# Channel mix of the skip path as 64-row products on both row halves of TensorE, with a new order of TensorE's and ScalarE's slots

## The reference

```
x_ft = rfft2(h); keep 12 x 12 low modes at both ends of the rows
x1 = irfft2(einsum("bixy,ioxy->boxy", x_ft, w))      # spectral path
x2 = einsum("bchw,oc->bohw", h, conv_w) + conv_b     # skip path: the channel mix
h  = layer_norm(x1 + x2); gelu in all but the last layer
```

## Time and profile before

| | us |
|---|---|
| median of 3 runs | 5614.82 (5611.42 to 5615.45) |
| the profiled execution | 5614.13 |
| its span in the trace | 5612.4 |
| stem phase, slots of `both`, head phase | up to about 810, 810 to 3280, 3280 to 4870 |
| attention and experts | 4900 to 5612 |

### The profile page before, as it was taken

The page is one execution under the profiler, slowest core; times in us unless marked ns, Lnnn a source line. Parts: engine busy times, 40 slices in busy tenths (PEclk is TensorE's granted clock), DMA queues, the critical chain, the costliest instruction groups (busy, mean ns, idle before and its releaser), DMA issues.

```text
span 5612.4 us, 134635 instructions
## 1 busy us (share of the span) xinstructions
PE 5147.1 (92%) x43556; PEld 2927.0 (52%) x43556; DVE 3916.8 (70%) x7712; ACT 3875.5 (69%) x6261; POOL 647.3 (12%) x959
## 2 busy tenths in 40 slices
PE   5878889999999999999999999999999999778778
PEld 2444456666666666666666644433333333334443
DVE  4877888888888888888888865555555554354454
ACT  5888776888666888666888666677777777523333
POOL 0133100233000333000332000000000000000000
PEclk9998899999999999999999999999999999878888
DMA  1334468667687667777676753221111111000000
GB/s 64 129 137 140 138 180 237 225 226 236 213 231 231 226 228 225 232 224 239 222 226 225 229 134 84 57 59 53 53 47 51 53 51 51 8 4 4 7 7 4
DMA packets 398465, 756.32 MB, mean 135 GB/s; under 512 B 246065, under 2 KB 304818, under 8 KB 332602
## 3 DMA queue, kind: packets, MB, share of 16 engines
q1 hardware_dynamic: 378170, 704.04, 39.4%
q0 software_dynamic: 19968, 48.01, 3.8%
HBM read 397.49 MB, written 354.42 MB: 134 GB/s over the span
## 4 chain that ended last, share of the span: by engine, by line
PE 70%; DVE 9%; ACT 8%; issue 7%; SPq 3%; DMA 3%; ACTq 1%; DVEq 0%
PE ps_y L926 10%; PE ps_t L938 8%; PE ps_t L1032 8%; PE ps_t L947 6%; PE ps_f L926 6%; PE ps_y L918 5%; PE ps_f L1017 4%; PE ps_s L903 3%; PE ps_t L1041 2%; PE ps_s L963 2%; DMA big<-hstore 2%; PE ps_t L353 2%; ACT wslot L1211 2%; PE ps_y L892 2%; PE ps_y L1002 2%
## 5 line engine op out<-in xcount | busy, mean ns | idle before, releaser
L1338 DVE TENSOR_REDUCE big<-big 128x16 f32<-128x512 f32 x1280 | 854.0, 675 | 685.3 <-ACT big L1176 681.0
L1331 DVE TENSOR_TENSOR big<-big 128x512 f32<-128x512 f32 x1280 | 938.7, 764 | 30.5 <-DVE big L1360 18.9
L1176 ACT ACTIVATE big<-ps_y 128x512 f32<-128x512 f32 x892 | 545.8, 612 | 482.7 <-PE ps_y L926 425.5
L938 PE MATMUL ps_t<-ident,big 128*128 128x128 f32 x5120 | 809.2, 281 | 55.2 <-DVE big L1331 25.1
L1192 ACT ACTIVATE big<-ps_t,g_now 128x512 f32<-128x512 f32 x1024 | 821.8, 803 | 12.1 <-PE ps_t L938 11.7
L926 PEld LDWEIGHTS ps_y<-conv_now,big 128*128 128x128 f32 x5088 | 616.3, 191 | 362.7 <-issue 362.7
L1185 ACT ACTIVATE big<-ps_t 128x512 f32<-128x512 f32 x1024 | 633.1, 618 | 212.8 <-PE ps_s L963 145.3
L938 PEld LDWEIGHTS ps_t<-ident,big 128*128 128x128 f32 x5120 | 576.1, 143 | 346.8 <-issue 304.6
L947 PE MATMUL ps_t<-ident,big 128*128 128x128 f32 x4096 | 655.5, 283 | 87.1 <-ACT big L1185 84.8
L926 PE MATMUL ps_y<-conv_now,big 128*128 128x128 f32 x5088 | 717.0, 284 | 0.0
L947 PEld LDWEIGHTS ps_t<-ident,big 128*128 128x128 f32 x4096 | 459.4, 143 | 282.0 <-issue 148.9
(11 more groups left out here) (197 smaller groups left out, 7238.6 us busy)
## 6 DMA issues: line engine op xcount, KB each, us to landing
hstore<-big SPq DMA_DIRECT2D x256, 1024.0 KB, 4.1
big<-hstore SPq DMA_DIRECT2D x256, 1024.0 KB, 5.3
xmodes<-x_out SPq DMA_DIRECT2D x128, 312.0 KB, 4.4
y_kt<-ymodes SPq DMA_DIRECT2D x512, 78.0 KB
ymodes<-y_st SPq DMA_DIRECT2D x192, 144.0 KB, 2.5
ymodes<-y_st SPq DMA_DIRECT2D x64, 192.0 KB, 3.3
w_raw<-in_tok_w1r POOLq DMA_DIRECT2D x128, 72.0 KB, 4.5
w_raw<-in_tok_w2r POOLq DMA_DIRECT2D x128, 72.0 KB, 4.4
```

The source lines that it names most:

```text
L938: last = nc.tensor.transpose(ps_t1[:, 128 * b:128 * b + 128], y_sb[2 * k + wh][:, 128 * b:128 * b + 128], ident[:, :])
L1176: af(y_sq[wh], of[:, wh, :], ACT.Square).then_inc(s["sq_done"], 1)
L1331: v_.tensor_tensor(groups(y_sb[2 * k + wh]), groups(y_sb[2 * k + wh]), rstd[:, k // 2, at:at + 16].unsqueeze(2).to_broadcast([128, 16, 32] ...
L1338: v_.tensor_reduce(ss[:, k // 2, at:at + 16], groups(y_sq[wh]), AX.X, ALU.add).then_inc(s["ss_done"], 1)
```

## The change

The channel mix is cut along the diagonal blocks of `conv_now`. `conv(pair, k, step, both)` now handles both units of a slot in two steps. In step 0 unit 0 is multiplied on rows 0 to 63 and unit 1 on rows 64 to 127, in step 1 the other way round. Each product has a 64 x 128 stationary and 64 moving columns and writes the matching 64 columns of its block. So within a step the two row halves write to two banks, and the two products of a block stand one behind the other in the program. Step 1 waits on a new semaphore `conv_half` for the end of step 0, and both `y_done` of a slot rise in step 1.

The slots' order changes with it. TensorE, with `both`: odd slots step 0, TB0, step 1, TO0, inv_w, [mode mix], TB1, TO1, [fwd_w]; even slots TB0, TO0, inv_h, TB1, step 0, TO1, step 1, fwd_h. ScalarE: even slots px0, gelu0, px1, gelu1, square0, keep0, square1, keep1; odd slots px0, gelu0, [sign_w2], square0, px1, gelu1, keep0, square1, keep1, [sign_w1, sign_w2]. `h_px` gets six buffers for four, and px waits for an earlier fwd_h. In head slots step 0 stands where conv 0 stood, and step 1 behind fc2(v,0) instead of behind fc2(v,1).

```diff
@@ -54,7 +54,7 @@
         h_new = [carve(2048) for _ in range(2)]
         y_sb = [carve(512) for _ in range(8)]
         y_sq = [carve(512) for _ in range(2)]
-        h_px = [carve(512) for _ in range(4)]
+        h_px = [carve(512) for _ in range(6)]
         ss, rstd = (carve(128).rearrange("p (j n) -> p j n", j=2) for _ in range(2))
         var, nt = carve(64), carve(64)
         t_w = carve(2048).rearrange("p (j n) -> p j n", j=2)
@@ -122,7 +122,7 @@
             "const_in", "const_zero", "fc0_center", "fc0_copied", "fc0_stored", "fc0_placed", "conv_center", "conv_placed",
             "pads_zero", "fc1_shift", "x_loaded", "x_ready", "x_turned", "x_copied", "conv_ready", "g_ready", "bias_ready",
             "h_loaded0", "h_loaded1", "h_stored0", "h_stored1", "y_loaded", "xmodes_stored", "ymodes_stored",
-            "y_done", "sq_done", "y_read", "ss_done", "norm_step", "xhat_done", "t1_done", "act_done", "t2_done",
+            "y_done", "conv_half", "sq_done", "y_read", "ss_done", "norm_step", "xhat_done", "t1_done", "act_done", "t2_done",
             "px_done", "f_done", "tw_done", "fw_done", "fw_read", "xout_done", "iw_done", "iw_read",
             "x_low", "x_high", "first_low", "first_high", "mix_done", "mix_sum", "mix_read", "w_raw", "w_zero", "w_scaled", "w_added",
             "xt_done", "fc1_done", "g1_done", "fc2_done", "g2_done", "fc3_done", "tok_done", "tok_stored0", "tok_stored1")}
@@ -328,6 +328,10 @@
         def y_of(odd, both):
 
             return ps_f if both and odd else ps_y
+
+        def px_room(k):
+
+            return 2 if k % 2 else 2 * k
 
         s_flat, f_flat = (t[:, :, :].rearrange("p a n -> p (a n)") for t in (ps_s, ps_f))
 
@@ -919,13 +923,21 @@
                                z_kx[j][r, :].rearrange("p (o w) -> p o w", w=32)[:, :, 16 * odd:16 * odd + 16],
                                start=True, stop=False)
 
-            def conv(k, wh, both):
-
+            def conv(pair, k, step, both):
+
+
+                if step == 1:
+                    wait(pe, "conv_half", pair + 1)
                 for b in range(4):
-                    at = 512 * (2 * (k % 2) + wh) + 128 * b
-                    last = mm(y_of(k % 2, both)[:, wh, 128 * b:128 * b + 128], h_in[k // 2][:, at:at + 128], conv_now[:, :],
-                              start=False, stop=(b == 3))
-                last.then_inc(s["y_done"], 1)
+                    for wh in range(2):
+                        r = slice(64 * (wh ^ step), 64 * (wh ^ step) + 64)
+                        at = 512 * (2 * (k % 2) + wh) + 128 * b
+                        last = mm(y_of(k % 2, both)[:, wh, 128 * b + r.start:128 * b + r.stop], h_in[k // 2][r, at:at + 128],
+                                  conv_now[r, r], start=False, stop=(b == 3 and step == 1))
+                        if b == 3 and step == 1:
+                            last.then_inc(s["y_done"], 1)
+                        elif b == 3 and wh == 1:
+                            last.then_inc(s["conv_half"], 1)
 
             def turn_out(unit, kind, k, wh, tok_before):
 
@@ -960,7 +972,7 @@
                         for image in range(2):
                             half, at = image ^ odd, 64 * image + 32 * wh
                             r = slice(64 * half, 64 * half + 64)
-                            last = mm(to[at:at + 32, odd, :], c_fwh[r, :], h_px[2 * odd + wh][r, :], start=True, stop=True)
+                            last = mm(to[at:at + 32, odd, :], c_fwh[r, :], h_px[px_room(2 * j + odd) + wh][r, :], start=True, stop=True)
                 last.then_inc(s["f_done"], 1)
 
             def fwd_w(m, iw_count, g1_count):
@@ -1072,8 +1084,12 @@
                     if inner:
                         head_slot(n, k, pair, turned, front, back2, kind, nxt, mixed, visit)
                         continue
+                    if both and k % 2 == 1:
+                        conv(4 * i + k, k, 0, True)
                     if back1 in STORED:
                         turn_back(turned - 2, k, 0)
+                    if both and k % 2 == 1:
+                        conv(4 * i + k, k, 1, True)
                     if kind is not None:
                         turn_out(turned, kind, (k + 1) % 4, 0, 0)
                     if front == "stem":
@@ -1084,10 +1100,6 @@
                         if isinstance(q, int) and q == 0 and k == 0:
                             pe.wait_ge(s["conv_ready"], ph)
                             wait(pe, "tw_done", 2 * n - 3)
-                        if k == 0:
-                            fwd_h(n - 2, 1, ps_s, 0, 2 * i + 1, 0, 0)
-                        if k == 2:
-                            fwd_h(n - 1, 0, ps_s, 0, 0, n - 1, 0)
                         if k % 2 == 0:
                             wait(pe, "mix_read", mixed)
                             inv_h(n, k, True)
@@ -1097,15 +1109,20 @@
                             inv_w(n + 1, 0, 0, 2 * n - 1, ps_s)
                         if visit is not None:
                             mix(*visit, ps_y, 2 * (4 * n + k))
-                        conv(k, 0, True)
                     if back1 in STORED:
                         turn_back(turned - 1, k, 1)
+                    if both and k % 2 == 0:
+                        conv(4 * i + k, k, 0, True)
                     if kind is not None:
                         turn_out(turned + 1, kind, (k + 1) % 4, 1, 0)
+                    if both and k % 2 == 0:
+                        conv(4 * i + k, k, 1, True)
+                        if k == 0:
+                            fwd_h(n - 2, 1, ps_s, 0, 2 * i + 1, 0, 0)
+                        else:
+                            fwd_h(n - 1, 0, ps_s, 0, 0, n - 1, 0)
                     if k == 1 and back2 in STORED and both:
                         fwd_w(n - 2, 2 * i + 2, 0)
-                    if front in MIXED:
-                        conv(k, 1, True)
                     if k == 1 and back2 in STORED and front == "stem":
                         fwd_w(n - 2, 0, 0)
                     if k == 2 and nxt in MIXED and front == "stem":
@@ -1139,14 +1156,14 @@
                 if not opening:
                     fc3(pair - 1, 2 * pair + 2)
                 if front is not None:
-                    conv(k, 0, False)
+                    conv(4 * i + k, k, 0, False)
                 fc2(v, 0)
+                if front is not None:
+                    conv(4 * i + k, k, 1, False)
                 fc1(v + 1, 1, iw_later, mixed if visit is None else mixed + visit[5])
                 if kind is not None:
                     turn_out(turned, kind, (k + 1) % 4, 0, pair)
                 fc2(v, 1)
-                if front is not None:
-                    conv(k, 1, False)
                 fc2(v + 1, 0)
 
             turn_x(0)
@@ -1182,7 +1199,7 @@
             def px(unit, k, wh, half):
                 act.wait_ge(s["t2_done"], unit + 1)
                 wait(act, "f_done", half)
-                af(h_px[2 * (k % 2) + wh], ps_t2[:, :], ACT.Copy).then_inc(s["px_done"], 1)
+                af(h_px[px_room(k) + wh], ps_t2[:, :], ACT.Copy).then_inc(s["px_done"], 1)
 
             def gelu(unit, m, k, wh, kind):
                 act.wait_ge(s["t1_done"], unit + 1)
@@ -1258,9 +1275,30 @@
                             square(unit + 1, 1, ps_y)
                             keep_y(unit + 1, k, 1, ps_y)
                         continue
+                    if front in MIXED and back1 in STORED:
+                        of = y_of(k % 2, True)
+                        px(turned - 2, k, 0, 2 * (n - 1) + (k - 1) // 2)
+                        if kind in STORED:
+                            gelu(turned, m, kt, 0, kind)
+                        if slots is not None and k == 3:
+                            sign_w2(ph, q - 8, slots[1], 1)
+                        if k % 2 == 1:
+                            square(unit, 0, of)
+                        px(turned - 1, k, 1, 2 * (n - 1) + (k - 1) // 2)
+                        if kind in STORED:
+                            gelu(turned + 1, m, kt, 1, kind)
+                        if k % 2 == 0:
+                            square(unit, 0, of)
+                        keep_y(unit, k, 0, of)
+                        square(unit + 1, 1, of)
+                        keep_y(unit + 1, k, 1, of)
+                        if slots is not None and k == 1:
+                            sign_w1(ph, q - 8, bass.ds(4 * q - 8 * 4 if slots[0] == 0 else 4 * q - 16 * 4, OCH), slots)
+                            sign_w2(ph, q - 8, slots[0], 0)
+                        continue
                     for wh in range(2):
                         if back1 in STORED:
-                            px(turned - 2 + wh, k, wh, 2 * (n - 1) + k // 2)
+                            px(turned - 2 + wh, k, wh, 2 * (n - 1) + (k - 1) // 2)
                         if kind in STORED:
                             gelu(turned + wh, m, kt, wh, kind)
```

## The result

The changed kernel takes 6356.5 us (median of four, 6333.4 to 6364.6) against 5613.2 us, a ratio of 1.132 (95% interval 1.129 to 1.135). The forecast was slower, which it is, but at 6136 us, and 6356 lies above its range of 5880 to 6300. The profiled execution has a span of 6359.4 us, 747 more than before's; 522 had been forecast.

What follows compares the result with a forecast made beforehand. TensorE, busy 92% and nearly gapless in the layers, was taken to bound the kernel. Scaling quads 219, other quads 127, head 126 and clock 50 sum to 522 us on 5614.13: 6136 us, range 5880 to 6300.

Steps and rivals of the forecast that it cites:

- The product: Channel mix step: 16 loads of 64x128 weights cost 0.89 us, as before, both halves loading at once; saving 0.
- rivals 1 and 2: Mix steps, 1: loads halve like streams, 5636 us, chance 0.05; 2: tiles also drain in half the time, 5480, chance 0.07.
- rival 3: Mix steps: the halves don't run at once, +0.89 us on each of 1024 steps, about 7000 us; chance 0.04.
- The chain and the shapes: Layer slots: waits of the new order and tile-shape changes, +219 us in 48 weight-scaling quads, +127 us in 49 others.
- the long wait: TensorE before TB1 of slot 2 in weight-scaling quads: px0 stands behind ScalarE's scaling block, 2.3 us.
- bare quad: Layer quad without weight scaling after the change: two halves of 13.32 us, 26.64 us in all.
- the small scaling: ScalarE in slot 3 of a scaling quad, ahead of the square: adds 0.25 us.
- shape changes: TensorE in layer quads: more switches between matmul tile shapes, 2.4 us a quad, 0 if waits hide them.
- The head: 124 head slots: y done later and fc2 waits for ScalarE, +1.0 us a slot, +126 us; between 0 and 1.2 a slot.
- The clock: Scaling quads: TensorE's wait lowers its granted clock, 1 us a quad, +50 us; up to +163 us.
- the bound of 3.4 a quad: Scaling quads: most clock loss allowed, from 6.8 us at 0.50 seen after one stem wait, 3.4 us a quad.
- the walk: Layer slots timed instruction by instruction along the new order: a scaling quad takes 29.2 us against 24.6.

Runs made afterwards that it cites:

- half-columns run: Changed kernel with each split product streaming 32 of its 64 columns, half of the channel mix's output columns left out, loads unchanged: 6335.2 us, 1.130.
- the order alone: Changed kernel's TensorE slot order and ScalarE order, with whole 128-row products where the split steps stood: 5944.7 us, 1.060 of the kernel before.
- the run with the wait taken away: Changed kernel with ScalarE's scaling block moved from the end of slot 1 to behind gelu 0 of slot 2: 6000.4 us, 1.069.
- the products alone: Kernel before, its slot and ScalarE order and old head kept, with split products in the layers at the two old places: 6924.9 us, 1.234.

## Why the forecast was right in direction and wrong in size

**The product: right.** A step is 0.97 us of loads, 1.04 with the shape change, in every clean stretch. That loads and not streams bind it is now shown, since halving the streams changed nothing; rivals 1 and 2 fall, and so does rival 3, as 16 loads fit where 8 did. "TensorEngine Tiling (Array Packing)" of the Trainium skill, section "Theoretical Speedup", gives up to twice the speed where a dimension is at most 64; the half-columns run shows why no part of it arrives here. "TensorE: Matmul & The Clock Gate" of the Trainium skill, section on LDWEIGHTS, has a load's time go with its columns and not with its rows; the trace agrees, with 0.97 for eight loads of 128 rows and for eight of 64 in each half.

**The chain and the shapes: right in sum, partly by luck.** Without the long wait the split kernel's scaling quad is 27.0 us; the forecast's bare quad with the small scaling is 26.64 + 0.25 = 26.9. Its mixing quads are 28.8, 2.7 above before (forecast 2.6). The wait adds 2.4 (forecast 2.3). Of the shape changes' 2.4 us a quad, 1.9 show in scaling quads and 1.2 in mixing ones (27.6 to 28.8): partly hidden. The reordering by itself cost more than I had given it: with whole products and no long wait a mixing quad grows by 1.5 (26.1 to 27.6), where the forecast less its shape changes leaves 0.2. The two errors cancel in the sum, and that is luck.

**The head: right.** 136 against 126. Before's second unit filled the gap in which fc2 waits for ScalarE, after's second step does not. Putting it back restores 1570 us.

**The clock: the step that failed.** "I take 1 us a quad" and the bound of 3.4 a quad. The loss is 33.9 - 29.2 = 4.7 us in each of 48 scaling quads, 226 us, and about 1.1 in each mixing quad, 50 us, where I took 50 in all and at most 163. The missing 225 us of the profiled sum are this. I took one event, 6.8 us at 0.50 in the stem, and used its length as the most that a wait can cause. In after the low stretch runs 13.6 us. Before's own trace already spoke against the bound: up to 810 us it has 25 such stretches of 3.4 to 10.2 us, and four of them are 10.2:

```profile
257.20:267.40 10.20, 9.56 (x65) 6.22 (x63) 7.33 (x9) 7.08 (x14) 6.55 (x9) 0.50 0.49 170
```

With 10.2 in place of 6.8 the bound would have been 5.1 a quad, above the 4.7 measured. The stem's stretches are also other work, with none of these products. And I gave the mixing quads no clock loss, though they have 2.2 us of low clock each.

**What is shown and what stays open.** Shown: at this length of wait, wait and split products together make the low clock. Filling the wait brings back 230 us, and that is clock alone, as work was added. Moving it brings back 356 and shortening it 310; by the walk the wait's own length is 115 and 58 of these. Whole products bring back 412, in which are the split's own 1.2 to 1.9 us a quad and the head's 23. Two waits of 1.2 and 1.1 us in a quad act nearly as one of 2.1. Not settled: what in the split products does it. TensorE's busy share before a fall (4.41 of 6.80 in after, 4.22 of 6.90 in the order alone, where it did not fall) does not tell the cases apart. Each fills half of the array's rows and streams half as many columns as before. The half-columns run halved the streams once more and had the same 12.7 us of low clock a scaling quad, so it does not hang on the streams from 64 columns down; 128 against 64 was not varied alone. Nor were the rows, the number of products (twice as many), or the moment at which y is done (a unit a step with whole products, both at step 1 with split ones). These stay open.

## What to carry to other kernels

Cost a product by its weight loads before you cut its streams: 64-row products on both halves load at the pace of the whole ones, so the split earned nothing, and its order and shape changes cost 7% even with the clock up (the run with the wait taken away). When a change both thins the work on TensorE and opens a wait of a microsecond or two in it, don't bound the clock's loss by one event elsewhere in the kernel: look at the longest low stretch in the trace, and fill or move the wait first and look at the granted clock (filling the wait alone gave back nearly 4% of the time). When you move a block of work on one engine, look at all that it sets off on the others; here that was GpSimd's sum behind it.

## What the runs showed of the chip that I had not expected

- The clock can stay at 0.50 through 13.6 us in which TensorE has no gap at all (1113.4 to 1127.0 in after), while with whole products in the same order nearly every low stretch ended after 3.4 us. It is no rule of split products as such: with the products alone 229 of the layers' 292 low stretches last 3.4 us, and before's stem, with whole products, has stretches of 10.2 us with TensorE busy for 9.56 of them.
- Two products whose results nobody reads made the kernel 230 us faster, by filling a 2.1 us wait.
- VectorE stood still for 1.56 of the 1.85 us of a GpSimd sum (the rows above). "SBUF — State Buffer" of the Trainium skill, section on the two separate sides, says that these two engines share ports by an exclusive lock for a whole instruction, also where VectorE only has two inputs in SBUF and GpSimd reads it; the trace agrees, with GpSimd first to start and both ends 0.07 us apart.
